# Lane attention's first tiles are loaded during the projections, and the split of Wo leaves each block's chain

## The reference

```python
x = x + jnp.tanh(g_xattn[0]) * window_attention(layernorm(x), ctx)     # stage 1
x = x + jnp.tanh(g_ffn[0])   * quantized_ffn(layernorm(x))             # stage 2, with the queries q
# second layer: k and v of ctx, of 16 heads of 16 channels of 4 lanes each
kh, vh = interfere(proj(ctx, Wk, bk)), interfere(proj(ctx, Wv, bv))    # stage 3: projections()
scores = einsum('bhqdm,bhkdm->bhqkm', qh, kh) / sqrt(dk)               # stage 4: lane_attention()
out = einsum('bhqkm,bhkdm->bhqdm', softmax(scores, axis=3), vh)
x = x + jnp.tanh(g_xattn[1]) * (out.reshape(b, s, dm) @ Wo.T + bo)
x = x + jnp.tanh(g_ffn[1])   * swiglu(layernorm(x))                    # stage 5
```

## Time and profile before

| what | value |
|---|---|
| median of 3 runs | 3434.41 us (3431.99 to 3435.84) |
| the profiled execution | 3426.74 us, span 3425.0 us, mean granted clock 0.972 |
| busy share of the span | PE 94%, PEld 72%, DVE 42%, ACT 26%, POOL 10% |
| last product of the projections starts | 1248.69 us |
| first PE instruction of lane attention | 1263.62 us |
| first maximum on DVE in batch 0, batch 1, batch 2, batch 3 | 1267.61, 1316.31, 1356.28, 1393.67 us |
| last store of lane attention issued; first instruction of the SwiGLU stage | 1909.63; 1914.38 us |

### The profile page before, as it was taken

One profiled execution on the slowest core, in us unless ns is written; L12 is line 12 of the kernel. 1 busy time (PEld: TensorE's weight loads), 2 busy tenths in 40 slices (PEclk: granted clock), 3 DMA queues, 4 the chain that ended last, 5 costly groups with the idle time before them and its releaser, 6 DMA issues. The chain is left out here.

```text
span 3425.0 us, 52086 instructions
## 1 busy us (share of the span) xinstructions
PE 3215.0 (94%) x20924; PEld 2472.3 (72%) x20924; DVE 1426.0 (42%) x2020; ACT 893.3 (26%) x1233; POOL 348.2 (10%) x304
## 2 busy tenths in 40 slices
PE   7999669998999978999999699999999999999999
PEld 4565537777788855666666588888888888778777
DVE  7888588872200017778877322122121222300000
ACT  3333343332211125545555211111111111200000
POOL 2000000000000012223222101111101100000000
PEclk9999789998999988999999899999999999999999
DMA  6776522212422232122211432222222222643443
GB/s 142 155 150 133 172 73 72 75 64 92 135 73 61 68 104 87 75 81 88 89 73 68 156 113 91 96 100 87 95 98 94 94 97 100 227 151 97 142 144 104
DMA packets 341751, 361.09 MB, mean 105 GB/s; under 512 B 154608, under 2 KB 261728, under 8 KB 339568
## 3 DMA queue, kind: packets, MB, share of 16 engines
q1 hardware_dynamic: 338160, 356.28, 33.0%
q10 hardware_dynamic: 3456, 2.90, 0.3%
HBM read 215.23 MB, written 135.36 MB: 102 GB/s over the span
## 5 line engine op out<-in xcount | busy, mean ns | idle before, releaser
L2290 PE MATMUL g_ps<-g_xs,g_wt 128*128 128x512 f32 x4128 | 949.6, 390 | 0.0
L2290 PEld LDWEIGHTS g_ps<-g_xs,g_wt 128*128 128x128 f32 x4128 | 775.4, 188 | 159.9
L2349 PE MATMUL g_ps<-g_wd,g_h 128*128 128x512 f32 x2016 | 463.4, 392 | 7.0 <-DMA g_h<-g_hidden 4.0
L2349 PEld LDWEIGHTS g_ps<-g_wd,g_h 128*128 128x128 f32 x2016 | 381.0, 189 | 88.8 <-DMA g_h<-g_hidden 5.3
L2206 DVE SCALAR_TENSOR_TENSOR g_act_out<-g_ps,g_g,g_act_out 128x512 f32<-128x512 f32 (+1 forms) x88 | 66.1, 751 | 672.8 <-ACT g_act_out L2139 672.7
L2139 ACT ACTIVATE g_act_out<-g_ps 128x512 f32<-128x512 f32 (+1 forms) x88 | 52.6, 597 | 634.5 <-PE g_ps L2290 634.4
L1325 PE MATMUL kv_gps<-kv_xh,kv_wh 128*128 128x512 f32 x512 | 201.9, 394 | 1.0 <-DVE kv_xl L1270 1.0
L1325 PE MATMUL kv_gps<-kv_xh,kv_wl 128*128 128x512 f32 x512 | 199.9, 390 | 0.0
L1325 PE MATMUL kv_gps<-kv_xl,kv_wh 128*128 128x512 f32 x512 | 199.8, 390 | 0.0
L1059 PE MATMUL f_gps<-f_xt,f_qwh 128*128 128x256 f32 x1024 | 192.1, 288 | 1.4 <-DVE f_xt L914 1.4
L2079 POOL TENSOR_TENSOR g_wt<-g_raw,g_wt 128x1024 fp32r<-128x1024 f32 x43 | 102.8, 2390 | 853.4 <-ACT g_wt L2116 853.4
(11 more groups left out here) (262 smaller groups left out, 4169.6 us busy)
## 6 DMA issues: line engine op xcount, KB each, us to landing
g_h<-g_hidden SPq DMA_DIRECT2D x176, 256.0 KB, 2.7
g_hidden<-g_h SPq DMA_DIRECT2D x84, 512.0 KB, 2.7
kv<-kv_y SPq DMA_DIRECT2D x16, 1024.0 KB, 5.7
a_kv<-kv SPq DMA_DIRECT2D x16, 1024.0 KB, 4.8
g_down<-g_raw SPq DMA_DIRECT2D x22, 512.0 KB, 2.8
g_raw<-g_down SPq DMA_DIRECT2D x22, 512.0 KB, 4.1
g_raw<-in_L_ffn_gate_w_dram SPq DMA_DIRECT2D x21, 512.0 KB, 3.9
g_raw<-in_L_ffn_up_w_dram SPq DMA_DIRECT2D x21, 512.0 KB, 3.9
```

The source lines that it names most:

```text
L2290: w = pe.matmul(gps[:, c % 2, m, :], wt[m][i][:, l, ks], xs[c][:, r, k, :], start=(k == 0 and a == 0), stop=(k == NK - 1 and a == 2))
L2349: w = pe.matmul(to, tile[:, p % RING, l, cols], wd[f][:, r, os], start=(f == 0 and a == 0), stop=False)
```

## The change

Tiles that both stages use are allocated once, around both (`lane_tiles`). In the projections' last part SP loads, ahead of the last two stores, the gate, batch 0's queries, its keys (the first half of `kv`) and the first four pieces of Wo, into tiles of the projections that are free by then; the second half of `kv` (the values) is loaded behind the wait for the last store. In lane attention the first four pieces of Wo are split ahead of batch 0's first block, the other four in the blocks c = 2, 3, 6 and 7 (`WO_AT`), with ACT's part one block earlier than DVE's. The output bias `gbo` is loaded behind Wo and scaled at block 7. POOL's zeroing of `va` leaves out the columns that are written anyway. x of batch 0 waits for 5 pieces instead of 8.

```diff
@@ projections, SP
                     load_w(2 * j + 2 + i, i)
                     store(2 * j + i, i)
+
+            sp.wait_ge(S["xt"], B)
+            sp.wait_ge(S["wp"], NB)
+            sp.wait_ge(S["low"], 1)
+            sp.dma_start(early["g"][:, 0:1], everywhere(gates[1:2], P)).then_inc(E["g"], 16)
+            sp.dma_start(early["q"], q_in[0]).then_inc(E["ql"], 16)
+            sp.wait_ge(S["out"], 16 * NK)
+            sp.dma_start(early["kv"][:, 0:NK, :], out[0][:, 0:NK, :]).then_inc(E["k0"], 16)
+            for k in range(4):
+                sp.dma_start(early["wo"][k][:, :], wot.rearrange("(k p) n -> k p n", p=P)[k]).then_inc(E[f"wo{k}"], 16)
             store(NB - 2, 0)
             store(NB - 1, 1)
             sp.wait_ge(S["out"], 16 * NB)
+            sp.dma_start(early["kv"][:, NK:2 * NK, :], out[0][:, NK:2 * NK, :]).then_inc(E["kvl"], 16)
@@ new function
+def lane_tiles(nc, ctx, columns):
+    s = Scope(nc, ctx, "early")
+    rows = s.sb("x", [P, 2, D])
+    raw = [s.sb(f"wraw{i}", [P, D]) for i in range(2)]
+    factors = s.sb("factors", [P, max(columns, D)])
+    tiles = {"x": rows, "wraw": raw, "factors": factors, "kv": s.sb("kv", [P, 2 * NK, P]), "g": s.sb("g", [P, 2]),
+             "q": factors[:, 0:D].rearrange("p (k t) -> p k t", t=P),
+             "wo": [rows[:, 0, :], rows[:, 1, :], raw[0], raw[1]]}
@@ lane_attention
+    WO_AT = {2: 4, 3: 5, 6: 6, 7: 7}
...
-        x = s.sb("x", [P, D])
-        xb = s.sb("xb", [P, D])
-        y = s.sb("y", [P, D])
-        yn = s.sb("yn", [P, D])
+        x, xb, y, yn = early["wo"]
@@ SP
-            load(0, 0)
-            for k in range(NK):
...
-            sp.wait_ge(S["wowl"], NK)
+            def load_wo(k):
+
+                sp.wait_ge(S["wowl"], k - 3)
+                sp.dma_start(early["wo"][k % 4][:, :], wot.rearrange("(k p) n -> k p n", p=P)[k]).then_inc(E[f"wo{k % 4}"], 16)
+
+            load_wo(4)
+            load_wo(5)
+            sp.wait_ge(S["kvl"], 16)
+            sp.wait_ge(S["ql"], 16)
+            load(1, 1)
+            load_wo(6)
+            load_wo(7)
+            sp.dma_start(gbo[:, :], everywhere(bo, P)).then_inc(S["consts"], 16)
+            sp.wait_ge(S["wowl"], 5)
             sp.dma_start(x[:, :], x_in[0]).then_inc(S["xl"], 16)
@@ POOL
-                pool.memset(va[i][:, :, :], 0.0).then_inc(S["ones"], 1)
-            pool.wait_ge(S["ones"], 2)
-            for i in range(2):
+                pool.memset(va[i][:, :, HD + 1:VW], 0.0).then_inc(S["ones"], 1)
@@ POOL, body and residual
-                pool.wait_ge(S["kvl"], 16 * b + 16)
+                if first:
+                    pool.wait_ge(E["k0"], 16)
+                else:
+                    pool.wait_ge(S["kvl"], 16 * b + 16)
...
+                if isinstance(n, int) and n == 0:
+
+                    pool.wait_ge(S["wowl"], NK)
@@ ACT
+            for k in range(4):
+                wo_high(k)
...
+                        if first and c + 1 in WO_AT:
+                            wo_high(WO_AT[c + 1])
+                        if first and c == NK - 1:
+                            act.wait_ge(S["consts"], 16)
+                            act.activation(gbo[:, :], gbo[:, :], ACT.Copy, scale=g[:, 1:2]).then_inc(S["gbo"], 1)
@@ DVE
+            for k in range(4):
+                wo_low(k)
             dve.wait_ge(S["ones"], 4)
...
+                        if first and c in WO_AT:
+                            wo_low(WO_AT[c])
```

More of the change, by code:

```diff
@@ L1094, with projections @@
 TOK = B * P
-def projections(nc, tag, x_in, w, bias, mixing, amp, out, left, right, out_left, out_right):
+def projections(nc, tag, x_in, w, bias, mixing, amp, out, left, right, out_left, out_right, early, E, gates, wot, q_in):
     jobs = [(a, o, (0, 1, 0)) for a, o in zip(left, out_left)] + [(a, o, (0, 0, 1)) for a, o in zip(right, out_right)]
@@ L1117, in projections @@
         xl = s.sb("xl", [P, NK, TOK], F32R)
-        wraw = [s.sb(f"wraw{i}", [P, D]) for i in range(2)]
+        wraw = early["wraw"]
         wh = [s.sb(f"wh{i}", [P, NK, P], F32R) for i in range(2)]
         wl = [s.sb(f"wl{i}", [P, NK, P], F32R) for i in range(2)]
-        x = s.sb("x", [P, 2, D])
+        x = early["x"]
         y = s.sb("y", [P, 2, TOK])
@@ L1129, in projections @@
         bmix = s.sb("bmix", [P, NB])
-        factors = s.sb("factors", [P, sum(widths)])
+        factors = early["factors"][:, 0:sum(widths)]
         parts = s.sb("parts", [P, 2, sum(widths)], F32R)
@@ L1344, in _, with lane_attention @@
             products(NB - 1, 1)
-def lane_attention(nc, q_in, kv_in, x_in, gates, wot, bo, x_out, norm_out):
+def lane_tiles(nc, ctx, columns):
[6 more added lines that the diff above has]
+             "wo": [rows[:, 0, :], rows[:, 1, :], raw[0], raw[1]]}
+    sems = {n: s.sem(n) for n in "g ql k0 kvl wo0 wo1 wo2 wo3".split()}
+    return tiles, sems
+def lane_attention(nc, early, E, q_in, kv_in, x_in, wot, bo, x_out, norm_out):
     U = 8
@@ L1369, in lane_attention @@
         wol = s.sb("wol", [P, NK, D], F32R)
-        q = [s.sb(f"q{i}", [P, NK, P]) for i in range(2)]
-        kv = [s.sb(f"kv{i}", [P, 2 * NK, P]) for i in range(2)]
+        q = [early["q"], s.sb("q1", [P, NK, P])]
+        kv = [early["kv"], s.sb("kv1", [P, 2 * NK, P])]
         va = [s.sb(f"va{i}", [P, NK * U, VW]) for i in range(2)]
@@ L1389, in lane_attention @@
         gbo = s.sb("gbo", [P, D])
-        g = s.sb("g", [P, 2])
+        g = early["g"]
         ident = s.sb("ident", [P, P])
@@ L1400, in lane_attention @@
         rflat = ring[:, :, :, :].rearrange("p s u t -> p s (u t)")
-        names = ("consts c1 um gate gbo wol wow wowl ones ql kvl km s vt ov w mx sub ex t te pv pve ot rcp on oh ol vaf xl xb res "
+        names = ("consts c1 um gate gbo wow wowl ones km s vt ov w mx sub ex t te pv pve ot rcp on oh ol vaf xl xb res "
                  "out stats aggr rstd yn ynout").split()
-        S = {n: s.sem(n) for n in names}
+        S = {n: s.sem(n) for n in names} | {"ql": E["ql"], "kvl": E["kvl"]}
         block = ctx.enter_context(nc.Block())
@@ L1457, in _ @@
         def _(sp):
-            sp.dma_start(g[:, 0:1], everywhere(gates[1:2], P)).then_inc(S["consts"], 16)
-            sp.dma_start(gbo[:, :], everywhere(bo, P)).then_inc(S["consts"], 16)
             def load(b, par):
@@ L1609, in _, with wo_low @@
             dve.tensor_reduce(um[:, :], um1[:, :, :, :].rearrange("p a d m -> p m (a d)"), AX.X, ALU.add).then_inc(S["um"], 1)
+            def wo_low(k):
+                dve.wait_ge(S["wow"], k + 1)
+                dve.scalar_tensor_tensor(out=wol[:, k, :], in0=early["wo"][k % 4][:, :], scalar=g[:, 1:2],
+                                         in1=woh[:, k, :], op0=ALU.mult, op1=ALU.subtract).then_inc(S["wowl"], 1)
+            for k in range(4):
+                wo_low(k)
             dve.wait_ge(S["ones"], 4)
@@ L2382, in gated_decoder @@
     stacks = [scratch(n + "_stack", (3 * rank, f.shape[1])) for n, f in zip(names, factors)]
-    projections(nc, "kv", cond, a["L1_xattn_Wkv"], a["L1_xattn_bkv"], mixing, amp, kv,
-                factors[:3], factors[3:], stacks[:3], stacks[3:])
-    lane_attention(nc, q, kv, x2, a["g_xattn"], a["L1_xattn_Wo"], a["L1_xattn_bo"], x3, x3n)
+    with ExitStack() as ctx:
+        tiles, sems = lane_tiles(nc, ctx, sum(f.shape[0] * f.shape[1] // P for f in factors))
+        projections(nc, "kv", cond, a["L1_xattn_Wkv"], a["L1_xattn_bkv"], mixing, amp, kv,
+                    factors[:3], factors[3:], stacks[:3], stacks[3:], tiles, sems, a["g_xattn"], a["L1_xattn_Wo"], q)
+        lane_attention(nc, tiles, sems, q, kv, x2, a["L1_xattn_Wo"], a["L1_xattn_bo"], x3, x3n)
     gate_a, up_a, down_a, gate_b, up_b, down_b = stacks
```

22 lines of the change are left out of this document (4 added, 18 removed).

## The result

| what | before | after |
|---|---|---|
| median of 4 runs each, same chip | 3433.2 us (3423.81 to 3435.84) | 3407.85 us (3397.87 to 3411.4) |
| ratio, with its 95% interval | | 0.9931 [0.9916, 0.9946] |
| the profiled execution | 3426.74 us, span 3425.0 us | 3397.87 us, span 3396.2 us, mean granted clock 0.974 |

The change gains 25.35 us by the medians.

A forecast was written before the change was run, and what follows sets the result against it. The prediction took DVE to set the pace in batch 0, waiting in each block for ACT's high part of Wo. Border 1.3 + batch 0 20.8 + batch 1 2.4 - clock 2.0 - scope 0.7 = 21.8 us, giving 3412.6, range 3406 to 3420.

The forecast's parts named there:

- Batch 0: Lane attention's first batch: DVE no longer waits for ACT's high part of Wo, 27.9 us instead of 48.70, gain 20.8.
- A block without Wo but with normalizing takes 3.03: Batch 0's blocks 4 to 7 were costed on DVE at 3.03 us, plus 1.20 in 6 and 7.
- In the blocks the low part starts first and POOL pays: In batch 0's blocks DVE's low part starts ahead of POOL's spread, which is delayed where POOL has slack.
- The border: Between projections and lane attention: early loads bring the first maximum sooner, gain 1.3 us, from 0 to 3.4.
- both give a first maximum near 1266.3: At the border, low parts and spreads taking turns, or POOL standing back, put the first maximum near 1266.3; gain 1.3.
- PE's clock: In batch 0 the lower granted clock slows only the first blocks: loss 2.0 us, range 0 to 10.4.
- Batch 1: Batch 0's residual, made earlier, no longer delays batch 1: gain 2.4 us of the 2.6 lost, 0.2 stay.
- The second scope: Between lane attention and SwiGLU the added scope's end costs a barrier and semaphore clearing: loss 0.7 us, 0 to 0.95.
- The clock staying low through batch 0: Rival: PE's clock stays at the lower level through batch 0, loss 10.4 instead of 2.0, time 3421.0; chance 0.10.
- a residual late in every batch: Rival, slower: each batch's residual comes late, batch 1's 2.6 us paid 15 times, time 3451.4; chance 0.02.
- no measurable change: Rival: low clock into batch 1 and values landing late, gain 0.9 us, time 3433.5; chance 0.04.
- The early loads bring nothing: Rival: the values land as late as before, the border's term is 0, time 3413.9; inside the range, no own chance.

The follow-up runs named there:

- e1_chain: Kernel after with its early loads, but all eight Wo splits back behind the exponentials of blocks 0 to 7; 3421.62 us, 0.9976 of before.
- e2_late: Kernel after with its order of splits, but nothing loaded early, all loads at the start of lane attention; 3410.78 us, 0.9936 of before.
- e7_nomax: Kernel after without the row maximum of the scores, 1.2 us of DVE's time in each block; 3394.32 us in one run.
- e8_turn6: Kernel after with six of PE's eight turnings in each block from batch 1 on; 3402.34 us in one run.
- e4_allin: Kernel after with one Wo split in each of the eight blocks and no low part in front; 3405.83 us, 0.9932 of before.
- e5_onein: Kernel after with the four front low parts made from one input, the high part's subtraction left out; first maximum 14.89 us after the last store.
- e9_again: Kernel after, unchanged, run once more; 3406.45 us against 3427.12 for before, 0.9940.
- e6_scope: Kernel before with an empty scope of eight semaphores around projections and lane attention; 3428.19 us beside 3431.93, one run of each.
- e11_vearly: Kernel after with batch 0's last value block stored and values loaded earlier, one low part in front, memsets behind the spreads; 3401.05 us, 0.9921 of before.
- e3_xlate: Kernel after with x of batch 0 loaded behind Wo's eighth low part instead of the fifth, as before; median 3406.97 us.
- e10_lateall: e2_late with e4_allin's order: no early loads, no low part in front; 3413.35 us against 3427.12 for before, 0.9955.

## Why the prediction was right, and where its sizes were off

**Batch 0, forecast 20.8, measured 21.3: right in place and size.** The mechanism is shown by the pair e1_chain (order back: 50.0) and e2_late (loads back: 27.4). Blocks came at 2.38, 2.39, 3.58, 3.58, 2.86, 2.85, 4.53, 5.22. Two sizes inside cancel. "A block without Wo but with normalizing takes 3.03" was read as DVE's time; it is 2.85, as e7_nomax and e8_turn6 show, so blocks 4 and 5 were cheaper. Against that, the low part of block 6 took 1.77, where an undisturbed one takes 1.27. My step "In the blocks the low part starts first and POOL pays" fails there: it starts at 1284.38, behind the start of POOL's spread at 1284.03, which keeps its 1.04, and DVE paid. In blocks 2 and 3 the low parts (1271.06 and 1274.64) started first, and the spreads beside them took 2.00 and 2.10.

**The border, forecast 1.3, measured 2.1.** The step "both give a first maximum near 1266.3" has the right mechanism: from the last store it is 15.6, forecast 16.4. Spreads took 3.82 instead of 2.08, low parts 2.47 and 4.04 instead of 2.56 each. The delay was 1.5 us for DVE, not the 2.1 of two whole spreads. The values landed 3.8 after their issue (1253.39 to 1257.21), between my 3.3 and 8.2, and weren't last: e4_allin copies them 10.9 us behind the store, after 14.4, so they were ready 3.5 earlier than DVE took them. The stage began 6.41 behind the store, forecast 6.43. The seven early transfers, costed at nothing, show no cost: the last store goes out at 1246.3 to 1253.3 us in the nine kernels that have them, and at 1248.5 to 1251.6 in the four without. By the Trainium skill, page "SBUF — State Buffer", section "SBUF: two separate sides", a DVE instruction with two SBUF inputs excludes a reading GpSimd one and memsets are spared; the rows of the kernel after agree (memsets of 0.90 and 0.93 us, 2.47 for two low parts beside them, then 3.82 and 4.04). The same section names a second kind of DVE instruction that takes the ports, one in a 2-port performance mode, against any GpSimd instruction. e5_onein's one-input instruction, at 743 ns and slowed by memsets, behaves like that kind; no trace here names its mode.

**PE's clock, forecast a loss of 2.0, measured 0 in batch 0.** The granted clock was 0.50 until 1269 and 0.99 from there, and DVE never waited for PE in batch 0. My step "I take the nearer end" was a choice between 0 and 10.4 and came out at the zero end. The Trainium skill, page "TensorE: Matmul & The Clock Gate", section "Part 1: The HAM clock gate (the "warmup" mystery)", lets sustained work bring the clock up. The rise at 1269 agrees, but the trace doesn't bear out sustained work as the whole of it: PE was busy for 4.66 of the 7.00 us ahead of the rise, and in the earlier trace rows for 10.08 of 12.00 at 0.50. So my choice of the near end came out right without a reason that the runs show. Yet 2.0 us went in the drain, of which I had said nothing: granted clock 0.66 after, 0.87 before, in the stretches shown. The kernels after, e2_late and e9_again have a drain of 66.5; before, e4_allin, e6_scope and e11_vearly 64.5; the others lie between (e8_turn6, with fewer turnings, aside). The instructions there are the same. In the 9.00 us ahead of the turning PE did the same in both, 87 instructions and 6.14 us at 1.00; then the clock was at 0.50 for 10.2 us after (from 1860.1) and for 3.4 us before (from 1892.7, 4 us later in its drain). It comes out alike in both traces of the kernel after, so it may hang on the moment at which the drain begins; what moves the clock there stays open.

**Batch 1, forecast 2.4, measured 3.3.** e3_xlate shows that the late x is the cause. What my working lacked is the second half of the loss, the lower clock behind PE's wait. The forecast kept 0.2 of the loss and measured against batch 2's 37.4. Batch 1 is now 0.8 shorter than batch 2: five of its blocks follow at 2.83 to 2.86, DVE's pace, where two of the kernel before and three of batch 5 take 3.03. PE is at 3.02 there already, as two of its score steps in batch 1 of the kernel after show:

```profile
1300.87 1.13 PE L1750 MATMUL a_ring<-a_km,a_q 64*128 64x512 f32 x4
...
1303.89 1.13 PE L1750 MATMUL a_ring<-a_km,a_q 64*128 64x512 f32 x4
```

DVE enters the batch late: its first maximum (1291.29) is 1.6 us behind the end of the scores, its sixth 0.5, and in the blocks of 3.03 of the later batches it is 0.05. So it catches up with PE in batch 1, and once only.

**The second scope, forecast 0.7, measured 0.4.** e6_scope has it alone.

**Rivals.** The clock staying low through batch 0 and a residual late in every batch are excluded by the rows above (batch 2 took 37.46, before 37.39), no measurable change by the interval of the ratio, which ends at 0.9946. "The early loads bring nothing" is false: 3.9 us with the same order (e4_allin against e10_lateall), and 1.6 by the low parts in front.

The sum: 2.1 + 21.3 + 3.3 + 0.1 - 2.0 - 0.4 = 24.4 against 21.8. The difference of 2.6 is border 0.8, batch 0 0.5, batch 1 0.9, scope 0.3 and 0.1 of later batches; the clock's term came out at the same 2.0 by chance, in another place. The rest up to 4.8 is no step of the prediction: the median of before is 1.2 lower than the one it started from, and 1.0 lies between the traces' 24.4 and the medians' 25.35.

## What to carry to other kernels

When an engine that works in order waits in each block for a short step of another one, move the step one block later before anything else: that brought 16 of the 23 us gained at the front of this stage, with no load moved ahead of it. Work in front of a stage costs nothing as long as the engine would wait there anyway; count that wait first. Before a pace read from a trace is used as an engine's cost, find out whose pace it is: two engines can both look nearly full, and leaving 1.2 us out of one of them told which it was, and in which blocks. And a gain in the median is not yet the edit's: of e11_vearly's 5.4 us the traces put 0.9 where the edit is.

## What the runs showed of the hardware

- A one-input DVE instruction of 743 ns (fp32, 128x1024, SBUF to SBUF) took 2.2 us beside POOL's memsets and 1.5 beside its spreads (e5_onein), while the two-input one of 1.27 us wasn't slowed by the same memsets.
- Of a low part and a spread that meet, the one that begins second seems to pay: 2.12, 2.00 and 2.10 instead of 1.04 for the spread, 1.77 instead of 1.27 for the low part, and 2.04 in e11_vearly, where it began 0.09 behind a spread that kept its 1.04.
- The granted clock of the drain differs between kernels with the same instructions there, by 2.0 us of time, though PE did the same in the 9 us ahead of it.
- A wait of PE of 2.0 us in batch 1 was followed by 3.4 us at a granted clock of 0.50, in the kernel before and in e3_xlate; without the wait the clock stayed at 1.00.
- An added scope with eight semaphores between two stages costs 0.4 us (e6_scope).
